# The last cross-attention's value product: one fp32 product or three single-pass products of split operands

## The reference

```python
x_   = layernorm(ctx);  lat = layernorm(x)
q    = lat @ Wq + bq                                   # inner width 1024: 16 heads of 64
kv   = concat([x_, lat], axis=1) @ Wkv + bkv           # 589 keys for 512 queries, per sequence
k, v = split(kv)                                       # then split into heads
sim  = einsum('bhid,bhjd->bhij', q * 64**-0.5, k)
sim  = sim - max(sim, axis=-1)
out  = einsum('bhij,bhjd->bhid', softmax(sim), v)      # 4 x 16 heads, 512 x 589 scores each
return out @ Wout + bout
```

## Time and profile before

| | us |
|---|---|
| runs shown | 1142.47, 1129.16, 1139.89 |
| median | 1139.89 |
| profiled execution | 1145.58 |
| its span, first to last instruction | 1143.9 |
| TensorE busy | 1060.7 (93%) |
| VectorE busy | 724.1 (63%) |
| ScalarE busy | 577.2 (50%) |
| GpSimd busy | 248.6 (22%) |
| mean granted TensorE clock | 0.941 |
| first and last exponential of the changed stage start | 425.7 and 1054.4 |

### The profile page before, as it was taken

The page is one execution under the profiler, slowest core; times in us unless marked ns, Lnnn a source line. Parts: engine busy times, 40 slices in busy tenths (PEclk is TensorE's granted clock), DMA queues, the critical chain, the costliest instruction groups (busy, mean ns, idle before and its releaser), DMA issues.

```text
span 1143.9 us, 14143 instructions
## 1 busy us (share of the span) xinstructions
PE 1060.7 (93%) x4746; PEld 734.1 (64%) x4746; DVE 724.1 (63%) x1640; ACT 577.2 (50%) x1057; POOL 248.6 (22%) x307
## 2 busy tenths in 40 slices
PE   6869999999999479999989999999999999999896
PEld 3648779888888256565657666676666676665532
DVE  5866575656656567768675776756767657752256
ACT  4336444342334345565554665646665646655453
POOL 6111220008447241212131111111111111110001
PEclk9978667999999679999999999999999999999998
DMA  7100000000001000000000000000000000000001
GB/s 230 7 1 1 1 1 1 1 1 1 1 1 37 1 1 1 1 1 0 1 1 1 1 1 1 1 1 1 1 1 1 1 1 1 1 1 1 1 0 38
DMA packets 15667, 9.87 MB, mean 9 GB/s; under 512 B 8760, under 2 KB 14828, under 8 KB 15084
## 3 DMA queue, kind: packets, MB, share of 16 engines
q1 hardware_dynamic: 15595, 8.96, 2.7%
HBM read 7.60 MB, written 1.05 MB: 8 GB/s over the span
## 4 chain that ended last, share of the span: by engine, by line
PE 85%; DVE 10%; ACT 3%; issue 1%; POOL 1%; POOLq 0%; DVEq 0%; ACTq 0%
PE PS L1459 81%; PE PS L1471 4%; DVE mxm L1349 1%; DVE st L988 1%; DVE X_ODD L999 1%; DVE X_EVEN L999 1%; DVE BIG L1082 1%; DVE mx L1079 1%; DVE QA L1292 1%; POOL rs L564 0%; DVE mv L991 0%; ACT BIG L725 0%; ACT BIG L717 0%; PE PS L1821 0%; DVE VXA L1308 0%
## 5 line engine op out<-in xcount | busy, mean ns | idle before, releaser
L1459 PE MATMUL PS<-BIG,VXA 128*128 128x512 f32 (+1 forms) x640 | 335.6, 606 | 0.0
L943 ACT ACTIVATE BIG<-PS 128x512 f32<-128x512 f32 (+1 forms) x320 | 189.7, 593 | 136.0 <-PE PS L1459 126.0
L1349 DVE TENSOR_REDUCE mxm<-PS 128x1 f32<-128x512 f32 x256 | 170.6, 687 | 95.7 <-PE PS L1459 91.1
L1459 PE MATMUL PS<-QA,KA 128*128 128x512 f32 (+1 forms) x320 | 194.8, 609 | 0.0
L1459 PEld LDWEIGHTS PS<-BIG,VXA 128*128 128x128 f32 (+1 forms) x640 | 115.2, 190 | 29.4 <-ACT BIG L943 8.5
L1459 PE MATMUL PS<-QB,KB 128*128 128x512 f32 (+1 forms) x320 | 126.2, 394 | 0.0
L1459 PE MATMUL PS<-KA,QA 128*128 128x512 f32 (+1 forms) x512 | 118.0, 333 | 8.0 <-DVE mxm L1349 7.0
L905 ACT ACTIVATE KA<-PS,b1s 64x78 fp32r<-64x78 f32 (+1 forms) x128 | 64.3, 502 | 90.9 <-PE PS L1459 89.2
L1459 PEld LDWEIGHTS PS<-KA,QA 128*128 128x128 f32 x512 | 86.5, 190 | 31.8 <-DVE mxm L1349 11.7
L666 POOL CAST KA<-KA 64x78 fp32r<-64x78 f32 (+1 forms) x128 | 55.0, 429 | 205.2 <-ACT KA L905 201.4
L666 POOL CAST QB<-QA 64x512 fp32r<-64x512 f32 x64 | 39.0, 609 | 268.8 <-ACT QA L905 268.6
(11 more groups left out here) (251 smaller groups left out, 1791.5 us busy)
## 6 DMA issues: line engine op xcount, KB each, us to landing
X_EVEN<-in_x SPq DMA_DIRECT2D x4, 256.0 KB, 3.3
VXA<-in_L_ffn_Wg SPq DMA_DIRECT2D x1, 1024.0 KB, 5.7
VXA<-in_L_ffn_Wu SPq DMA_DIRECT2D x1, 1024.0 KB, 7.7
VXA<-in_L_ffn_Wd SPq DMA_DIRECT2D x1, 1024.0 KB, 9.3
REG<-in_L_xattn_Wkv SPq DMA_DIRECT2D x1, 1024.0 KB, 4.7
QB<-crow SPq DMA_DIRECT2D x64, 2.0 KB
out<-X_EVEN SPq DMA_DIRECT2D x4, 256.0 KB, 2.3
wq1s<-in_L_xattn_Wq SPq DMA_DIRECT2D x1, 512.0 KB, 8.5
```

Source lines behind the costliest of these rows:

```text
L943: act.activation(PX[0:rows, g % 4, :], PS[0:rows, g % 2, :], ACT.Exp, scale=SCALE_W).then_inc(pw_ready, 1)
L1349: dve.tensor_reduce(mxm[:, p % 2, h, m:m + 1], PS[:, 2 + g % 2, :], AX.X, ALU.max).then_inc(mu_free, 1)
L1459: return pe.matmul(dst, lhsT, rhs, start=start, stop=stop, **kw)
```

## The change

The exponentials and the values get a leading part of type fp32r and a rest, and `pv` becomes three single-pass products, rest of V by leading P, leading V by leading P, leading V by rest of P. PX stays and is the whole exponential. The leading part PHI is made in slots 0, 1, 4, 5, 6 and 9 by ScalarE, which takes the exponential out of the bank a second time right behind the first; in slots 2, 3, 7 and 8 by VectorE, as a copy of PX at the end of its slot (`lead`). The rest PLO is PX - PHI, made by GpSimd in every slot (`rest`), in place over PX, behind the slot's twin copies, with a wait for its own result. `pv` runs two slots behind the scores (LAG), not one, and waits for the leading part; its third product waits for the rest.

V is projected by quarters of the width (four heads, 256 columns) for each key block, so 80 projections instead of 40: the next quarter's in slots 2, 7, 8 of an even step and 2, 7 of an odd one. ScalarE makes their leading part (`value_lead`, behind the slot's exponentials and `hi`, ahead of `head_sums`), VectorE the rest (`value`). The buffers VHI and VLO hold two quarters each, with ones beside the leading parts and zeros beside the rests. The maxima units are spread anew, units 0 and 1 into slots 8 and 9 of the step before; the row of maxima goes to slot 7 and "yE" to slot 8.

```diff
@@ -183,8 +183,23 @@
 STEPS = PAIRS
+LAG = 2
 HEAD_SLOTS = {2: 1, 7: 0}
-MAX_UNITS = {0: [0], 1: [1, 2], 2: [3, 4], 3: [5, 6], 4: [7], 5: [8, 9]}
+MAX_UNITS = {0: [2], 1: [3], 2: [4], 3: [5], 4: [6], 5: [7, 8], 6: [9], 8: [0], 9: [1]}
+LEAD_ON_VECTOR = (2, 3, 7, 8)
+
+
+def max_units(p, slot):
+
+    first = p + 2 if slot > 7 else p + 1
+    return [(first, u) for u in MAX_UNITS.get(slot, []) if first < PAIRS]
+
+
+def leads(g):
+
+    p, slot = divmod(g, SLOTS)
+    on_vector = len(LEAD_ON_VECTOR) * p + sum(s <= slot for s in LEAD_ON_VECTOR)
+    return g + 1 - on_vector, on_vector
 OD_STEPS = {(0, 8): (1, 0), (0, 9): (1, 1), (2, 9): (2, 0), (3, 9): (2, 1), (5, 9): (3, 0), (6, 9): (3, 1)}
@@ -198,15 +213,14 @@
     if p + 2 < PAIRS:
         t[0], t[3], t[5] = [("Q", p + 2)], [("K", p + 2)], [("Kt", p + 2)]
     if p + 1 < PAIRS:
-        t[6] = [("c", p + 1)]
+        t[7] = [("c", p + 1)]
     b, hp = divmod(p, NHP)
-    half, step = divmod(hp, HALF)
-    if b + half < B:
-        for slot, j in ((2, 2 * step), (7, 2 * step + 1)):
-            if j < KB:
-                t[slot] = [("V", b + half, 2 * j + 1 - half)]
+    ahead = p // 2 + 1
+    if ahead < B * QUARTERS:
+        for j, slot in ((0, 2), (1, 7), (2, 8)) if p % 2 == 0 else ((3, 2), (4, 7)):
+            t.setdefault(slot, []).append(("V", ahead, j))
     if b and hp == 0:
-        t[6].append(("yE", b - 1))
+        t[8].append(("yE", b - 1))
     for slot in range(8, SLOTS):
         if (p, slot) in OD_STEPS:
...
-PROLOGUE = ([("Q", 0), ("K", 0), ("Kt", 0), ("soft",), ("V", 0, 0), ("max", 0), ("max", 1), ("V", 0, 2), ("max", 2), ("max", 3),
-             ("V", 0, 4), ("max", 4), ("max", 5), ("V", 0, 6), ("max", 6), ("max", 7), ("V", 0, 8), ("max", 8), ("max", 9),
-             ("qT", 2), ("c", 0), ("kv", 2), ("Q", 1), ("qT", 3), ("K", 1), ("kv", 3), ("Kt", 1)])
+PROLOGUE = ([("Q", 0), ("K", 0), ("Kt", 0), ("soft",), ("V", 0, 0), ("max", 0, 0), ("max", 0, 1), ("V", 0, 1), ("max", 0, 2), ("max", 0, 3),
+             ("V", 0, 2), ("max", 0, 4), ("max", 0, 5), ("V", 0, 3), ("max", 0, 6), ("max", 0, 7), ("V", 0, 4), ("max", 0, 8), ("max", 0, 9),
+             ("qT", 2), ("c", 0), ("kv", 2), ("Q", 1), ("qT", 3), ("K", 1), ("kv", 3), ("Kt", 1), ("max", 1, 0), ("max", 1, 1)])
...
+
+        VHI, VLO = (over(name, vxa_at + 4 * 2 * KB * 2 * 3 * DW * n, [P, 2, KB, 2, 3, DW]) for n, name in enumerate(("VHI", "VLO")))
+        PHI, PLO = over("PHI", vxa_at + 4 * 2 * 2 * KB * 2 * 3 * DW, [P, 4, S]), over("PLO", big_at, [P, 4, S])
...
@@ -649,7 +666,8 @@
             split_wide(6)
             pool.wait_ge(v_full, LV["down", B - 1, E] + 1)
             pool.wait_ge(v_full, LV["kv", 1] + 1)
-            settled(pool.memset(VX[:, :, :, 1, :], 1.0))
+            for values, fill in ((VHI, 1.0), (VLO, 0.0)):
+                settled(pool.memset(values[:, :, :, :, 1, :].rearrange("p r j c d -> p (r j c) d").bitcast(F32), fill))
             def twins(key):
...
+            def rest(g):
+
+                p, slot = divmod(g, SLOTS)
+                rows = min(P, KEYS - P * (slot % KB))
+                pool.wait_ge(pw_ready, g + 1)
+                if slot in LEAD_ON_VECTOR:
+                    pool.wait_ge(lead_dve, leads(g)[1])
+                else:
+                    pool.wait_ge(lead_act, leads(g)[0])
+                pool.tensor_tensor(PLO[0:rows, g % 4, :], PX[0:rows, g % 4, :], PHI[0:rows, g % 4, :].bitcast(F32), ALU.subtract).then_inc(rest_ready, 1)
+                pool.wait_ge(rest_ready, g + 1)
+
             for key in PROLOGUE:
...
@@ -687,6 +717,7 @@
                     for key in step_tasks(p).get(slot, []):
                         if key[0] in ("Q", "K", "Kt"):
                             twins(key)
+                    rest(SLOTS * p + slot)
                     if p in LAT_STEPS:
...
+            def value_lead(key):
+
+                _, ahead, j = key
+                n = PJ[key]
+                rows = min(P, KEYS - P * j)
+                if ahead == 0 and j == 0:
+                    act.wait_ge(setup_done, N_E_OPERANDS)
+                if ahead >= 2 and j == 0:
+                    act.wait_ge(pv_ready, SLOTS * 2 * (ahead - 1))
+                act.wait_ge(pj_full, n + 1)
+                act.activation(VHI[0:rows, ahead % 2, j, :, 0:3:2, :],
+                               PS[0:rows, 6 + n % 2, 0:4 * DW].rearrange("p (c n d) -> p c n d", c=2, n=2), ACT.Copy).then_inc(vhi_ready, 1)
+
...
@@ -941,8 +987,13 @@
                     if g >= 4:
                         act.wait_ge(pv_ready, g - 3)
                     act.activation(PX[0:rows, g % 4, :], PS[0:rows, g % 2, :], ACT.Exp, scale=SCALE_W).then_inc(pw_ready, 1)
+                    if slot not in LEAD_ON_VECTOR:
+                        act.activation(PHI[0:rows, g % 4, :], PS[0:rows, g % 2, :], ACT.Exp, scale=SCALE_W).then_inc(lead_act, 1)
                     for key, h in splits(tasks, slot):
                         hi(key, h)
+                    for key in tasks.get(slot, []):
+                        if key[0] == "V":
+                            value_lead(key)
                     if slot in HEAD_SLOTS and 2 * p - HEAD_SLOTS[slot] >= 0:
                         head_sums(2 * p - HEAD_SLOTS[slot])
...
@@ -1294,19 +1345,13 @@
                     ins.then_inc(pj_free, 1)
             def value(key):
-                _, b, u = key
+                _, ahead, j = key
                 n = PJ[key]
-                j, half = divmod(u, 2)
                 rows = min(P, KEYS - P * j)
-                if b == 0 and u == 0:
-                    dve.wait_ge(setup_done, N_E_OPERANDS)
-                if b and u == 0:
-                    dve.wait_ge(pv_ready, SLOTS * (NHP * b - NHP // 2))
-                if b and u == 1:
-                    dve.wait_ge(pv_ready, SLOTS * NHP * b)
-                dve.wait_ge(pj_full, n + 1)
-                dve.tensor_copy(VX[0:rows, j, HALF * half:HALF * half + HALF, 0:3:2, :],
-                                PS[0:rows, 6 + n % 2, :].rearrange("p (c n d) -> p c n d", c=HALF, n=2)).then_inc(pj_free, 1)
+                dve.wait_ge(vhi_ready, KB * ahead + j + 1)
+                dve.tensor_tensor(VLO[0:rows, ahead % 2, j, :, 0:3:2, :],
+                                  PS[0:rows, 6 + n % 2, 0:4 * DW].rearrange("p (c n d) -> p c n d", c=2, n=2),
+                                  VHI[0:rows, ahead % 2, j, :, 0:3:2, :].bitcast(F32), ALU.subtract).then_inc(pj_free, 1)
             def c_rows(key):
...
+            def lead(g):
+
+                rows = min(P, KEYS - P * (g % KB))
+                dve.wait_ge(pw_ready, g + 1)
+                dve.tensor_copy(PHI[0:rows, g % 4, :], PX[0:rows, g % 4, :]).then_inc(lead_dve, 1)
...
@@ -1376,9 +1427,8 @@
             for p in range(STEPS):
                 tasks = step_tasks(p)
                 for slot in range(SLOTS):
-                    if p + 1 < PAIRS:
-                        for u in MAX_UNITS.get(slot, []):
-                            maxima(p + 1, u)
+                    for unit in max_units(p, slot):
+                        maxima(*unit)
                     if slot - 1 in HEAD_SLOTS and 2 * p - HEAD_SLOTS[slot - 1] >= 0:
                         head_out(2 * p - HEAD_SLOTS[slot - 1])
                     for key, h in splits(tasks, slot - 1):
@@ -1396,6 +1446,8 @@
                     for key in tasks.get(slot, []):
                         if key[0] not in ("Q", "K", "Kt"):
                             task(key)
+                    if slot in LEAD_ON_VECTOR:
+                        lead(SLOTS * p + slot)
             head_out(2 * PAIRS - 1)
             dve.wait_ge(cn_in, N_CN)
@@ -1742,7 +1794,10 @@
...
                 if g >= 2:
-                    pe.wait_ge(pw_ready, g - 1)
+                    if (slot - 2) % SLOTS in LEAD_ON_VECTOR:
+                        pe.wait_ge(pw_ready, g - 1)
+                    else:
+                        pe.wait_ge(lead_act, leads(g - 2)[0])
                 dst = PS[0:rows, g % 2, :]
                 mm(dst, KA[r][h][:, P * j:P * j + rows], QA[r][h][:], stop=False)
...
@@ -1753,14 +1808,20 @@
                 b, hp = divmod(p, NHP)
                 head = 2 * p + h
                 rows = min(P, KEYS - P * j)
-                pe.wait_ge(pw_ready, g + 1)
+                if slot in LEAD_ON_VECTOR:
+                    pe.wait_ge(lead_dve, leads(g)[1])
+                else:
+                    pe.wait_ge(lead_act, leads(g)[0])
                 if j == 0 and head >= 2:
                     pe.wait_ge(on_ready, head - 1)
-                if j == 0 and h == 0 and hp == 0:
-                    pe.wait_ge(pj_free, PJ["V", b, 2 * KB - 2] + 1)
-                if j == 0 and h == 0 and hp == HALF:
-                    pe.wait_ge(pj_free, PJ["V", b, 2 * KB - 1] + 1)
-                mm(PS[:, 4 + h, :], value_and_ones(j, hp, h, rows), PX[0:rows, g % 4, :], start=j == 0, stop=j == KB - 1).then_inc(pv_ready, 1)
+                if j == 0 and h == 0 and p % 2 == 0:
```

(49 more changed lines are left out.)

## The result

The changed kernel takes 1324.9 us (four runs, 1324.3 to 1326.6) against 1141.2 for the kernel before: a ratio of 1.165, 95% interval 1.156 to 1.174. A kernel also has slower executions at a lower clock, so the ratios here compare only the faster ones of each kernel, while the medians take all. The forecast was 1260, range 1190 to 1310. The direction was right, and so were the waits that it named; the size was not, 184 us instead of 121.

The account below looks back on a forecast made before the run. TensorE's own work was taken as the bound. Products -51, value projections +8, waits behind twins +129, Kt +9, slot 8 +26 sum to +121: 1267 for the profiled execution, 1260 us as median; range 1190 to 1310.

Parts of the forecast that it names:

- What bounds the kernel, and where the wait arises: Last cross-attention: TensorE's own work sets a step; it would wait behind Q's and K's twins, +129 us.
- The chain's size: Q's second head, twin copy, then rest on GpSimd: TensorE sees rest(0) at A+4.88, is there at A+2.66, stands 2.2 us.
- The step's period: One step of the stage, a pair of heads in ten slots: some 22.8 us, TensorE standing about 5.3 of it.
- The clock falls too: TensorE's granted clock falls to 0.9 on average around the waits, 58 us in all, giving 1290 to 1315; chance 0.13.
- Rival 2: TensorE's granted clock also falls, to 0.9 on average, adding 1.9 us a step: 1290 to 1315; chance 0.13.
- Slot 8: Third pass of values 8 waits behind V's leading part and the head's logarithm and exponential: 0.7 to 1.0 us, +26 us.
- Kt's wait: Slot 5: third pass of values 5 waits for rest(5) behind Kt's evacuations and copies: 0.3 us a step, +9 us.
- No engine is over TensorE, so totals alone would say a gain: Per step: TensorE needs 17.6 us, ScalarE 16.3, GpSimd 15.6, VectorE 15.4; only the order of queues makes a loss.
- Dense products would give 1097: Rival that TensorE stays dense, the third pass finding its rest ready: -51 + 8, so 1097 us; chance 0.05.
- the copy reckoned at 0.55: VectorE's leading copy inside SBUF, four a step, taken at 0.55 us each in VectorE's total of 15.4.
- Rival 4: Leading copies and rests block each other, two copies a step at slots 7 and 8, +39 us: 1299; chance 0.06.

Follow-up runs that it names:

- no rest waited for: Changed kernel with the third product multiplying the leading exponentials again instead of their rest, rests still computed: 1159.2 us against 1146.9 for the kernel before.
- the best of all versions: Changed kernel, rests before twins, leading copies and head sums first, third product a slot later, twins by DMA except first two pairs': 1136.7 us, ratio 0.989.

## Why the prediction was wrong

*What bounds the kernel, and where the wait arises: right.* Two stands a step behind the twins, at values 0 and 3. The forecast had 60 of 2.2 and 2.1 us, the trace has 54 of 1.6 us or more. Taking the twins out of the rests' way returned 140 of 184 us, the clock's part with them.

*The chain's size: right.* Forecast A+1.99, 2.80, 3.51, 4.88; measured A+1.87, 2.68, 3.37, 4.69. The second exponential starts 0.48 behind the first and not 0.60, and TensorE sees a rest 0.04 us after its end and not 0.10. TensorE is there at A+2.76, forecast 2.66. So 1.93 us stand against 2.2.

*The step's period: right at full clock.* Forecast about 22.8; 22.91 and 22.46 where the stands are filled. The stage at full clock is 761.4 - 628.7 = 133 us longer, against the forecast 121 for the whole; what makes the other 12 was not separated.

*The clock: the step that failed.* The sum put it at nothing, and "The clock falls too" got 0.13. It measured 38 us of the stage, and 41 of the time where the stands were filled. Of the 65 us between forecast and result 38 are this term, 12 the rest of the stage, 8 lie ahead of the stage and behind it, and 6 are the step from the profiled execution to the median, which the sum took off and which the changed kernel doesn't have; 1 is rounding. The row that I quoted for it, 0.73 in the window after a wait of 1.45 us, was the evidence, and I named two longer waits in every step, 60 in all. To leave such a fall as a rival was the mistake: it belonged in the sum. The forecast with it, 1260 + 41 to + 58, is 1301 to 1318, still short of 1324.9. The range's end of 1310 had taken the clock in only as an edge. Rival 2 had the fall itself right: it took 0.9 for the mean clock, and the stage has 0.89.

*Slot 8: too large, as far as one step tells.* It came out at about 0.35 in the step above (the third product at 816.05, its second pass issued at 815.47), forecast 0.7 to 1.0. Kt's wait cannot be told from its neighbours there.

*"No engine is over TensorE, so totals alone would say a gain": wrong, and hidden by the stands.* Dense products would give 1097, I wrote; 1159 was measured with no rest waited for, and 1136.7 is the best of all versions. The totals left out, among other things, what two engines do to each other: the copy reckoned at 0.55 took 0.80 in the mean with no rest waited for. How much of the 62 us that explains was not separated. Here a copy of 0.42 took 1.45 beside a run of rests. The Trainium skill ("SBUF — State Buffer", section "Who interferes with whom") says that whichever of such a pair issues first has the shared ports for its whole instruction, and the other is blocked until then; the trace agrees, as the copy that began at 714.30 ended only 0.28 us behind the run of rests (715.75 against 715.47). Rival 4, the blocking, did not have the time of the changed kernel: its copies averaged 0.47.

## What to carry to other kernels

When an engine gets a new operation in every slot, write down what stands ahead of it in that engine's program and in which slot that was made: a lag in slots covers the new operation only if nothing ahead of it belongs to a later slot. If the forecast has TensorE stand for 2 us again and again, take a lower clock into the sum, from a row where it was seen, and don't leave it to a rival; filling the stands with products of zeros then tests what it costs. And reckon that one engine's load can lengthen another's operations: here taking copies from GpSimd made VectorE's copies shorter.

## What the runs showed of the hardware

- Behind all 27 long stands behind K's twins TensorE ran for several us at the lower clock (0.53 to 0.76 over 7 us), behind Q's, as long, only ten times of 27. Products of zeros in the stands brought the stage from 0.89 to 0.99 and made the kernel 41 us faster for 118 us of added work.
- A VectorE copy of 128x512 inside SBUF took 0.40 us at its shortest and up to 1.47 where GpSimd was busy with subtractions, which in turn had a median of 1.28 and took up to 1.90 (with no rest waited for).
- Twin copies moved from GpSimd to DMAs (all 192, or the 180 of the later pairs) landed a median of 2.2 to 2.3 us after issue for 128 KB, at 34 GB/s in the windows. With all 192 the waits view has TensorE wait for them twice, 4.4 us in all; with 180 it has no such wait.
